# A group's rotary queries moved to its head, and a cached attention whose mix is computed turned

## What is computed

```python
kv_c = kv @ W_kvc
q_c = q @ W_dq
q_nope = (q_c @ W_uq).reshape(b, lq, H, HD).transpose(0, 2, 1, 3)
q_rope = (q_c @ W_qr).reshape(b, lq, H, R).transpose(0, 2, 1, 3)
k_nope = (kv_c @ W_uk).reshape(b, lk, H, HD)
v = (kv_c @ W_uv).reshape(b, lk, H, HD)
q_rope = _rope(q_rope, lq)
scores = (einsum('bhqd,bkhd->bhqk', q_nope, k_nope) + einsum('bhqr,bkr->bhqk', q_rope, k_rope)) * scale
out = einsum('bhqk,bkhd->bqhd', softmax(masked scores), v).reshape(b, lq, H * HD) @ W_o
```

```python
k = concatenate([k_cache, x @ wk]);  v = concatenate([v_cache, x @ wv])
out = einsum('bqk,bkd->bqd', softmax((x @ wq) k^T * scale), v) @ wo
x = x + tanh(g_xattn[3]) * out
```

## Time and profile before

| what | value |
|---|---|
| median of three runs | 2584.8 us (2584.8 to 2590.09) |
| the profiled execution, its own time | 2584.63 us |
| its span in the trace | 2582.9 us |
| TensorE busy | 2366.0 us, 92% of the span |
| VectorE, ScalarE, GpSimd busy | 1044.0, 648.3, 381.8 us |
| granted TensorE clock, mean | 0.96 of full speed |

### The profile page before, as it was taken

The page is one execution under the profiler, slowest core; times in us unless marked ns, Lnnn a source line. Parts: engine busy times, 40 slices in busy tenths (PEclk is TensorE's granted clock), DMA queues, the critical chain, the costliest instruction groups (busy, mean ns, idle before and its releaser), DMA issues. The chain is left out here.

```text
span 2582.9 us, 34785 instructions
## 1 busy us (share of the span) xinstructions
PE 2366.0 (92%) x10386; PEld 1387.5 (54%) x10387; DVE 1044.0 (40%) x2555; ACT 648.3 (25%) x1415; POOL 381.8 (15%) x528
## 2 busy tenths in 40 slices
PE   7898989999888899999999998789999999699898
PEld 4444444444665566666556654245656655345486
DVE  5545454545333434435612223772222222702375
ACT  2444444441111334443111110210111111051221
POOL 6000000000212100000011113501111112500061
PEclk9999999999999999999999999799999999899999
DMA  9401010003775100000536664152444452551220
GB/s 327 122 1 33 0 33 0 0 25 119 222 234 166 32 10 10 18 14 1 171 110 199 199 199 122 48 164 78 142 155 140 157 165 73 158 200 36 85 86 29
DMA packets 170887, 263.70 MB, mean 102 GB/s; under 512 B 13328, under 2 KB 106896, under 8 KB 170287
## 3 DMA queue, kind: packets, MB, share of 16 engines
q1 hardware_dynamic: 139821, 185.96, 22.7%
q0 software_dynamic: 16000, 49.30, 6.7%
q10 hardware_dynamic: 14976, 27.27, 2.8%
HBM read 212.68 MB, written 49.81 MB: 102 GB/s over the span
## 5 line engine op out<-in xcount | busy, mean ns | idle before, releaser
L1157 PE MATMUL bank<-f2r_wd,f2b_hT 128*128 (+1 forms) x300 | 137.2, 593 | 1.4 <-DVE f2b_hT L1261 1.4
L1138 PE MATMUL bank<-f2r_wg,f2b_xT 128*128 x400 | 129.2, 467 | 1.8 <-ACT f2b_xT L1194 1.6
L1138 PE MATMUL bank<-f2r_wu,f2b_xT 128*128 x400 | 126.5, 459 | 0.0
L1594 PE MATMUL bank<-l0a_vo,l0a_zT 128*112 128x512 f32 x256 | 115.5, 594 | 2.9 <-DVE l0a_zT L1752 2.9
L1564 PE MATMUL bank<-l_kvcT,xnT 128*112 128x375 f32 x256 | 98.5, 508 | 20.7 <-DVE l0a_qrT L1724 20.7
L1248 DVE TENSOR_TENSOR f2b_h<-bank,f2b_acted 128x352 f32<-128x352 f32 x50 | 26.2, 525 | 202.5 <-PE bank L1138 202.5
L1655 ACT ACTIVATE l0a_p<-l0a_p,l0a_low 112x375 f32<-112x375 f32 x128 | 77.1, 607 | 115.3 <-DVE l0a_low L1745 114.2
L1735 DVE CUSTOM_DVE_ANT_0 l0a_p<-bank,xn 112x375 f32<-112x375 f32 x128 | 70.3, 549 | 71.4 <-PE bank L1566 40.6
L1138 PEld LDWEIGHTS bank<-f2r_wu,f2b_xT 128*128 128x128 f32 x400 | 76.2, 190 | 42.6 <-issue 0.5
L1919 PEld LDWEIGHTS bank<-l1w_v,ctxT 128*125 128x125 f32 x768 | 86.2, 187 | 17.4 <-issue 17.4
L2472 POOL TENSOR_SCALAR f_below<-l_raw,l_half 128x512 f32<-128x512 f32 x33 | 58.4, 1784 | 237.0 <-POOLq L286 200.4
(11 more groups left out here) (410 smaller groups left out, 4457.0 us busy)
## 6 DMA issues: line engine op xcount, KB each, us to landing
slot_rows<-zeros SPq DMA_DIRECT2D x2, 7424.0 KB, 42.1
slot_rows<-f2b_y ACTq DMA_DIRECT2D x50, 256.0 KB, 3.8
f1r_wg<-in_l_wg SPq DMA_DIRECT2D x16, 704.0 KB, 4.5
f1r_wu<-in_l_wu SPq DMA_DIRECT2D x16, 704.0 KB, 6.3
f2r_wg<-in_l_wg SPq DMA_DIRECT2D x16, 704.0 KB, 4.5
f2r_wu<-in_l_wu SPq DMA_DIRECT2D x16, 704.0 KB, 6.3
xn<-in_l_w_ffn SPq DMA_DIRECT2D x11, 768.0 KB, 4.3
l_raw<-in_l_w_ffn SPq DMA_DIRECT2D x11, 768.0 KB, 4.2
```

The source lines that it names most:

```text
L1138: mm = pe.matmul(bank[:, 0:width], xT[:, v, k, :], w[:, bass.ds(at, 1), k, :].rearrange("p o f -> p (o f)"), start=(k == 0), stop=(k == KD ...
L1157: mm = pe.matmul(bank_y[v][:, :], hT[0:fn, v, c, :], wd[0:fn, bass.ds(at, 1), c, :].rearrange("p o f -> p (o f)"), start=(c == 0), stop=(c ...
L1594: mm = pe.matmul(s.bank[7][0:TOK, :], zT[:, b % 2, j, :], vo[:, j, :], start=(j == 0), stop=(j == GH - 1))
```

## The change

In the first attention the rotary queries come first in a group and go into banks 0 to 3, which the scores of the group before have left; half by half, so that the first two banks are complete before the second half starts. The products of weights go to banks 4 to 7 (`qk0` in 4, `vo` in 5, 6, 7, 4, `qk1` in 5), and the other queries to banks 6, 7, 4 and 5; each of these now waits for the copy out of the bank that it takes. The SP queue fetches the next group's weights when the weight products of this one are done.

In the cached attention the mix is computed turned: 128 columns of the values are the weights, the 112 columns of `pT` move, and four such slices stand side by side in one bank. So the step `turn_mix` and the tile `z` fall away, ScalarE copies the mix as `zT`, and the division is put into the last addition, whose factor is now `share` = 1/total times the gate. The steps on TensorE are four, one round less; the projections alternate between banks 6 and 7. On VectorE the addition comes ahead of the reciprocal.

```diff
-        qr_banks = (6, 7, 0, 1)
+        vo_banks = (5, 6, 7, 4)
+        q_banks = (6, 7, 4, 5)
...
-                sp.wait_ge(qr_done, g * QR + 1)
+                sp.wait_ge(w_done, g * W_DONE - W_DONE + 2 + GH)
...
             with pe.Fori(0, NG) as g:
                 pe.wait_ge(loaded, (g + 1) * 96)
+                pe.wait_ge(s_masked, 1 + g * N)
+                for half in range(2):
+                    for jj in range(2):
+                        pe.matmul(s.bank[2 * half + jj][:, 0:HALF], w_qr0[:, jj * 128:(jj + 1) * 128],
+                                  a.qcT0[:, halves(half)], start=True, stop=False)
+                    for jj in range(2):
+                        pe.matmul(s.bank[2 * half + jj][:, 0:HALF], w_qr1[row_group(jj), :],
+                                  a.qcT1[row_group(jj), halves(half)], start=False, stop=True).then_inc(qr_done, 1)
...
+                pe.wait_ge(y_added, 1 + g * B)
                 for j in range(GH):
-                    pe.matmul(s.bank[2 + j][:, :], w_uv[:, j, :], w_o[:, j, :], start=True, stop=True).then_inc(w_done, 1)
+                    if j == GH - 1:
+                        pe.wait_ge(w_copied, g * W_COPIES + 1)
+                    pe.matmul(s.bank[vo_banks[j]][:, :], w_uv[:, j, :], w_o[:, j, :], start=True, stop=True)\
+                      .then_inc(w_done, 1)
+                pe.wait_ge(w_copied, g * W_COPIES + 2)
...
-                pe.wait_ge(y_added, 1 + g * B)
-                pe.wait_ge(w_copied, g * W_COPIES + 2 + GH)
...
-                        if half:
-                            pe.wait_ge(w_copied, g * W_COPIES + 2 + GH + j + 1)
-                        pe.matmul(s.bank[2 + j][:, 0:HALF], qk0[:, j, :], a.qcT0[:, halves(half)],
+                        pe.wait_ge(w_copied, g * W_COPIES + (2 + GH + j + 1 if half else 3 + j))
+                        pe.matmul(s.bank[q_banks[j]][:, 0:HALF], qk0[:, j, :], a.qcT0[:, halves(half)],
...
-                for t in range(KT):
-                    pe.matmul(s.bank[4 + b % 2][0:TOK, :], pT[:, b % 2, t, :], vc[:, b % 2, t, :],
-                              start=(t == 0), stop=False)
-                pe.matmul(s.bank[4 + b % 2][0:TOK, :], pT[0:TOK, b % 2, KT, :], vn[:, b, :],
-                          start=False, stop=True).then_inc(z_done, 1)
...
-            def turn_mix(b):
...
+                for m in range(KD):
+                    out, of = s.bank[4 + b % 2][:, m * TOK:(m + 1) * TOK], slice(m * 128, (m + 1) * 128)
+                    for t in range(KT):
+                        pe.matmul(out, vc[:, b % 2, t, of], pT[:, b % 2, t, :], start=(t == 0), stop=False)
+                    mm = pe.matmul(out, vn[:, b, of], pT[0:TOK, b % 2, KT, :], start=False, stop=True)
                 mm.then_inc(zt_done, 1)
...
-                if b:
-                    pe.wait_ge(y_added, b)
+                if b >= 2:
+                    pe.wait_ge(y_added, b - 1)
...
-            for n in range(B + 4):
-                for lag, step in enumerate((scores, turn, mix, turn_mix, project)):
+            for n in range(B + 3):
+                for lag, step in enumerate((scores, turn, mix, project)):
...
-                    dve.tensor_scalar(z[:, b % 2, :], s.bank[4 + b % 2][0:TOK, :], inv[:, b % 2:b % 2 + 1], None,
-                                      ALU.mult).then_inc(z_scaled, 1)
...
+                    dve.scalar_tensor_tensor(out=s.x[:, b, :], in0=s.bank[6 + b % 2][0:TOK, :],
+                                             scalar=share[:, b % 2:b % 2 + 1], in1=s.x[:, b, :],
+                                             op0=ALU.mult, op1=ALU.add).then_inc(y_added, 1)
```

More of the change, by code:

```diff
@@ L1613, in _ @@
[L1613 to L1620, removed]
@@ L1627, in _ @@
                     for j in range(GH):
-                        pe.matmul(s.bank[2 + j][:, 0:HALF], qk1[row_group(j), j // 2, :],
+                        pe.matmul(s.bank[q_banks[j]][:, 0:HALF], qk1[row_group(j), j // 2, :],
                                   a.qcT1[row_group(j), halves(half)], start=False, stop=True).then_inc(w_done, 1)
@@ L1673, in _ @@
                 act.wait_ge(w_done, g * W_DONE + 1)
-                act.activation(qk0[:, :, :], s.bank[0][:, 0:GH * KVC].rearrange("p (h n) -> p h n", h=GH),
+                act.activation(qk0[:, :, :], s.bank[4][:, 0:GH * KVC].rearrange("p (h n) -> p h n", h=GH),
                                ACT.Copy).then_inc(w_copied, 1)
@@ L1683, in _ @@
                     act.wait_ge(w_done, g * W_DONE + 2 + GH + i + 1)
-                    act.activation(qT[:, i % GH, halves(i // GH)], s.bank[2 + i % GH][:, 0:HALF],
+                    act.activation(qT[:, i % GH, halves(i // GH)], s.bank[q_banks[i % GH]][:, 0:HALF],
                                    ACT.Copy).then_inc(w_copied, 1)
@@ L1708, in rotate @@
                 half, jj = i // 2, i % 2
-                bank = s.bank[qr_banks[i]]
+                bank = s.bank[i]
                 def tokens(ap):
@@ L2233, in cache_attention_stage @@
         inv = sb("inv", [TOK, 2])
+        share = sb("share", [TOK, 2])
         pT = sb("pT", [TT, 2, KT + 1, TOK])
-        z = sb("z", [TOK, 2, D])
         zT = sb("zT", [128, 2, KD, TOK])
@@ L2320, in project @@
                 pe.wait_ge(zt_copied, b + 1)
-                if b:
-                    pe.wait_ge(y_added, b)
+                if b >= 2:
+                    pe.wait_ge(y_added, b - 1)
                 for k in range(KD):
-                    mm = pe.matmul(s.bank[7][0:TOK, :], zT[:, b % 2, k, :], w_o[:, k, :],
+                    mm = pe.matmul(s.bank[6 + b % 2][0:TOK, :], zT[:, b % 2, k, :], w_o[:, k, :],
                                    start=(k == 0), stop=(k == KD - 1))
@@ L2353, in _ @@
                                        accum_out=t.magnitudes[:, m, c:c + 1]).then_inc(sized, 1)
-            for n in range(B + 3):
+            for n in range(B + 2):
                 if n < B:
@@ L2365, in _ @@
                     if b >= 2:
-                        act.wait_ge(z_done, b - 1)
+                        act.wait_ge(zt_done, b - 1)
                     act.activation(pT[:, b % 2, 0:KT, :],
@@ L2394, in _ @@
             dve.tensor_tensor(t.output_scale[:, :], t.scale[:, 2:3], s.tanh_g[:, 7:8], ALU.mult)
-            for n in range(B + 5):
+            for n in range(B + 3):
                 if n < B:
@@ L2421, in _ @@
                     of.aggregate(dve, b, b + 1)
+                if 0 <= n - 1 < B:
+                    b = n - 1
+                    dve.wait_ge(e_done, b + 1)
+                    if b >= 2:
+                        dve.wait_ge(y_added, b - 1)
+                    dve.reciprocal(inv[:, b % 2:b % 2 + 1], total[:, b % 2:b % 2 + 1]).then_inc(inv_done, 1)
+                    dve.wait_ge(inv_done, 2 * b + 1)
+                    dve.tensor_tensor(share[:, b % 2:b % 2 + 1], inv[:, b % 2:b % 2 + 1], s.tanh_g[0:TOK, 3:4],
+                                      ALU.mult).then_inc(inv_done, 1)
 def ternary_ffn_stage(nc, s, d, t):
```

44 lines of the change are left out of this document (15 added, 29 removed).

## The result

The changed kernel takes 2556.09 us (median of four runs, 2552.78 to 2559.47), the kernel before 2584.8: a ratio of 0.9886, 95% interval 0.9866 to 0.9907. The prediction was 2555.9. The profiled execution took 2556.08 us, its span is 2554.3.

A forecast was written before the change was run, and what follows sets the result against it. TensorE, busy 92% of the span, was taken as the bound, its largest wait in the touched stages being for VectorE's rotation (20.7 us). Savings 16.8 + 8.2 + 2.2 + 1.5 = 28.7 us from 2584.63 gave 2555.9, range 2550 to 2567.

The forecast's parts named there:

- head of a group: First attention, group start to scores: 21.3 us instead of 25.54, saving 4.2 a group, 16.8 over four groups.
- rotation, from the group's start: VectorE's rotation of the queries in a group's head: starts at about 2.7 us, ends at 18.4, 2.9 before needed.
- what ends last in the head: Before a group's scores: ScalarE's last query copy, at 21.3 us, is late next; TensorE's pause shrinks from 5.18 to about 1.2.
- clock behind the pause: Start of a group's scores: granted clock 1.00 instead of 0.50, saving 2.04 us a group, 8.2 over four.
- mix, a round: Cached attention: 32 records at 0.111 us, 3.55 us instead of 3.83, saving 0.28 a round, 2.2 over eight.
- waits for the last bank: End of the cached attention: two waits for shared bank 7, 1.5 us together, go.
- third rival: Cached mix: weight loads not hidden, 0.29 us a record, 9.2 a round, kernel slower at 2601 us; chance 0.03.
- The addition ahead of the reciprocal: VectorE in cached rounds: done 1.9 us into a round, before scores end at 3.31, so cost 0; unhidden, up to 1.9.
- second rival: Cached mix: moving columns alone set the pace, 0.0975 us a record, 3.12 a round, kernel 2552.4 us; chance 0.10.

The follow-up runs named there:

- e3: The kernel before, with five matmuls of no use put into TensorE's wait for the rotation at a group's head; 2578.59 us (ratio 0.9967).
- e6: The changed kernel with one bank instead of two for all projections of the cached attention; 2561.31 us.
- e4: The changed kernel with the same weights but only 56 of the 112 columns moving in the turned mix; 2560.68 us.
- e5: The changed kernel, the first sequence's scores waiting only for the query copies and rotations they read or whose banks they overwrite; 2553.7 us, repeated 2556.52.
- second comparison: The changed kernel unaltered, run again beside the kernel with early scores; 2557.98 us.

## Why the prediction was right

| step | predicted | measured in the changed kernel |
|---|---|---|
| head of a group | 21.3 us, saving 4.2 | 21.46, saving 4.08; four times 16.3 |
| rotation, from the group's start | 2.7 to 18.4 | 2.65 to 18.31 |
| what ends last in the head | ScalarE's last copy, pause about 1.2 | the copy, pause 1.26 |
| clock behind the pause | 1.00, saving 2.04 a group | 1.00, saving 2.03 at the first scores (e3: 2.02), 2.25 by the group's length (e3) |
| mix, a round | 3.55 | 3.57; saving 0.26, eight times 2.1 |
| waits for the last bank | 1.5 | gone; 1.86 by what is left of the stage; one of the two costs 1.17 (e6) |

The sum of 28.7 us stands against 29.06 by the stages. *The head:* the size of this term hung on who ends next to last, and that could be read from the copies of before. The other queries start 10.32 us after the group (10.3 in the sum) and ScalarE's last copy ends 11.01 later (11.02); that the scores start only 0.13 after that copy is what the sum left out.

The two terms of the first attention can be told apart by the length of a group, from its start to the next one's or, for the last, to the table load. The last three groups repeat from run to run: on the mean one takes 123.48 us in before, 117.16 in the changed kernel and 121.23 in e3. So the change saves 6.32 a group, the clock alone 2.25, and the difference, 4.07, is the head's 4.08.

*The clock:* the term was taken from one row of before, a wait of 1.0 us that left 1.00 behind it, against one of 5.18 that left 0.50. The 2 us were not lost again later in the body: the stage gave 25.1, where the head alone would give 16.3. e3 shows the term alone, and that it was put 0.2 us a group too low: that much of the saving comes only behind VectorE's first release, at which the term was read.

*The mix:* the choice between 0.0975 and 0.113 a record was made by the longer weight load, and e4 shows that this was the right reason: with 56 moving columns it still is 0.110. The third rival, loads that are not hidden, is out by the rows: loads of 192 ns at a pace of 0.1116 us. The Trainium skill (TensorE: Matmul & The Clock Gate, Part 3, "The mechanism"), on whose rule it stood, lists that a load overlaps a running matmul only if their row groups differ. For these matmuls of 112 and 125 rows that does not hold: with loads that are not hidden the mix would have taken 9.2 us a round. Ahead of that list the same section also lets a load into the background weight buffer be pulled ahead of running matmuls. The rows do not speak against that case, which the prediction did not weigh.

*The last bank:* of the cached attention's 3.94 us the mix gives 2.1, and 1.86 are left, more than the 1.5 of the two waits. In before these were

```profile
2429.06 3.66 PE L2324 MATMUL bank<-l3w_o,l3a_zT 128*112 128x512 f32 x8 [0.55 <-DVE x L2417]
2433.66 3.66 PE L2324 MATMUL bank<-l3w_o,l3a_zT 128*112 128x512 f32 x8 [0.94 <-DVE x L2417]
```

e6 brings back the second alone, and with it 0.23 us of lost overlap that the prediction did not count. The first stands behind `turn_mix`, which is gone; no run shows it by itself.

*The addition ahead of the reciprocal* cost nothing, as reckoned: in the cached rounds VectorE is through 1.35 us before the next scores are there:

```profile
2381.49 0.16 DVE L2417 TENSOR_TENSOR l3a_share<-l3a_inv,tanh_g 112x1 f32<-112x1 f32 x1
2383.01 0.67 DVE L2397 TENSOR_REDUCE l3a_top<-bank 112x1 f32<-112x487 f32 x1 [1.35 <-PE bank L2289]
```

What the prediction did not have is the spread of the untouched part, which alone moves single runs by more than the difference between the forecast and its second rival. That 2555.9 met 2556.09 so closely is partly luck; the stages are what bears the steps out.

## What to carry to other kernels

Where one engine waits for a long job of another, order its own work so that the job's input comes first, and ask then what ends next to last: that, and not the wait, is the gain. A wait can cost twice, once as idle time and once as the lower clock behind it; a few matmuls of no use, put into the wait, tell the second price alone. Count a gain by the stage and also by what follows it: e5 won 5.3 us in one stage and gave about 6 back in the next.

## What was not expected of the hardware

The granted clock falls not only behind a pause like the 5.18 us of before. In the routing of the changed kernel it fell while TensorE was working, in a run with a pause of only 0.28 us ahead of it (L520 at 583.60); and in e5 it stayed at the low level through 17 us of unbroken work. At the end of the third layer's feed-forward part it went with the length of a wait for gathered rows. Two lines, the first of the kernel before, the second of the changed kernel in its second comparison:

```profile
2226.18 10.89 PE L956 MATMUL bank<-f_shared_d,f2c_hT 128*112 128x512 f32 x24 [1.88 <-DVE x L1030]
```

```profile
2203.41 13.10 PE L956 MATMUL bank<-f_shared_d,f2c_hT 128*112 128x512 f32 x24 [4.84 <-DVE x L1030]
```

The windows (with the busy times of PE, PEld, DVE, ACT and POOL, then granted clock, DMA share, GB/s) show the clock in each, of before and then of the other:

```profile
2226.20:2231.20 5.00, 5.00 (x12) 1.95 (x12) 4.06 (x6) 0.00 (x0) 4.00 (x4) 1.00 0.56 153
```

```profile
2203.40:2208.40 5.00, 4.99 (x6) 1.98 (x7) 4.05 (x6) 0.00 (x0) 3.97 (x4) 0.50 0.57 154
```

With the wait longer by 3.0 us, the work behind it took 2.2 more. The same holds in all eleven profiles: behind the seven waits of 4.18 to 4.88 us the next 5 us are granted 0.50, behind the four of 1.05 to 1.88 they are granted 1.00. VectorE waits there for transfers of gathered rows, and how long differs from execution to execution. This is a part of why the untouched part spreads as it does, but can't be all of it: the changed kernel's first profile has a wait of 4.86 and one of the shortest untouched parts. The rest of that spread was not traced.
